# Attention 2: one slot for the keys and values of both token tiles, the key turn one slot sooner, weight transfers behind three swaps

## The reference

```python
x = x + _layernorm(_L0_attn_ref(_layernorm(x, axis=-1), ...), axis=-1)
x = x + _layernorm(_L0_ffn_ref(_layernorm(x, axis=-1), ...), axis=-1)

# in _L0_ffn_ref, for hidden states of 4 batches x 256 tokens x 256:
q = (h @ Wq).reshape(B, S, NH, HD)       # NH = 32 query heads of HD = 128
k = (h @ Wk).reshape(B, S, KVH, HD)      # KVH = 4 key heads
v = (h @ Wv).reshape(B, S, KVH, HD)
q = _rope(q, pos)                        # x1*cos - x2*sin, x1*sin + x2*cos on the two halves
k = _rope(k, pos)
scores = jnp.einsum('bqhd,bkhd->bhqk', q, k) / jnp.sqrt(jnp.float32(HD))   # k, v repeated for 8 query heads each
attn = jax.nn.softmax(where(causal, scores, -1e9), axis=-1)
o = jnp.einsum('bhqk,bkhd->bqhd', attn, v).reshape(B, S, NH * HD) @ Wo
# then: router, top 8 of 32 experts, gated experts and a shared expert
```

## Time and profile before

| | |
|---|---|
| time, median of 3 runs | 948.99 us (947.24 to 949.40) |
| profiled execution, its own time | 950.87 us |
| span of the profiled execution | 948.8 us |
| busy share of the span: PE, PEld, DVE, ACT, POOL | 91%, 85%, 65%, 60%, 48% |
| attention 2: start of its program, first scores, scores of slot 60 | 184.2, 200.45, 598.55 us |
| mean granted TensorE clock | 0.97 |

### The profile page before, as it was taken

The page is one execution under the profiler, slowest core; times in us unless marked ns, Lnnn a source line. Parts: engine busy times, 40 slices in busy tenths (PEclk is TensorE's granted clock), DMA queues, the critical chain, the costliest instruction groups (busy, mean ns, idle before and its releaser), DMA issues. The chain is left out here.

```text
span 948.8 us, 18792 instructions
## 1 busy us (share of the span) xinstructions
PE 867.5 (91%) x6108; PEld 802.1 (85%) x6108; DVE 616.5 (65%) x1620; ACT 570.5 (60%) x1570; POOL 455.9 (48%) x486
## 2 busy tenths in 40 slices
PE   5799998767999999999999999978999999999994
PEld 4699897657999998999899999867888888888884
DVE  5456667647787787778777777755444544544546
ACT  6788888656766766667666667654333333433333
POOL 3743334357867766777776777720222222221221
PEclk9799999978999999999999999997999999999998
DMA  7001000131114111421111111200433333333321
GB/s 234 1 1 46 22 23 1 59 93 39 35 46 142 38 45 35 114 66 46 34 46 35 46 45 36 51 1 18 144 116 116 114 98 115 101 114 116 112 82 45
DMA packets 50246, 63.34 MB, mean 67 GB/s; under 512 B 5728, under 2 KB 36064, under 8 KB 50176
## 3 DMA queue, kind: packets, MB, share of 16 engines
q1 hardware_dynamic: 49088, 61.41, 22.2%
q10 hardware_dynamic: 1088, 1.05, 0.3%
HBM read 41.86 MB, written 1.18 MB: 45 GB/s over the span
## 5 line engine op out<-in xcount | busy, mean ns | idle before, releaser
L639 POOL TENSOR_TENSOR b_prob<-b_prob,b_rsum 128x256 f32<-128x256 f32 (+1 forms) x128 | 104.7, 839 | 108.3 <-DVE b_rsum L621 108.3
L73 PE MATMUL banks<-act_t,b_w 128*128 128x256 f32 (+1 forms) x392 | 129.3, 330 | 3.9 <-DVE b_work L1194 2.8
L74 PE MATMUL banks<-act_t,b_w 128*128 128x256 f32 (+1 forms) x392 | 127.2, 324 | 0.0
L75 PE MATMUL banks<-act_t,b_w 128*128 128x256 f32 (+1 forms) x392 | 127.0, 324 | 0.0
L1955 ACT ACTIVATE moe_hid<-banks 128x512 fp32r<-128x512 f32 x66 | 39.5, 598 | 124.1 <-DVE banks L2046 124.1
L1355 ACT ACTIVATE b_prob<-banks,b_negmax 128x128 f32<-128x128 f32 (+1 forms) x256 | 103.6, 416 | 13.3 <-DVE b_negmax L1342 12.9
L2039 DVE TENSOR_TENSOR moe_gated<-banks,moe_share 128x512 f32<-128x512 f32 x66 | 45.6, 691 | 85.0 <-PE banks L75 80.9
L1211 ACT ACTIVATE b_qt<-b_work 128x512 fp32r<-128x512 f32 x64 | 40.5, 632 | 97.5 <-POOL b_work L1206 97.5
L639 POOL TENSOR_TENSOR a_prob<-a_prob,a_rsum 128x256 f32<-128x256 f32 x64 | 52.0, 834 | 82.2 <-DVE a_rsum L621 82.2
L1206 POOL TENSOR_TENSOR b_work<-b_work 128x512 f32<-128x512 f32 x64 | 86.7, 1355 | 9.2
L1202 POOL TENSOR_TENSOR b_work<-b_work,rope_t 128x512 f32<-128x512 f32 x64 | 84.2, 1315 | 8.2 <-DMA b_work<-b_work 8.2
(11 more groups left out here) (237 smaller groups left out, 3026.0 us busy)
## 6 DMA issues: line engine op xcount, KB each, us to landing
b_work<-b_work SPq DMA_DIRECT2D x128, 128.0 KB, 2.3
moe_share<-gates SPq DMA_DIRECT2D x32, 512.0 KB, 3.6
b_w_raw<-in_b_wq SPq DMA_DIRECT2D x4, 1024.0 KB, 5.5
b_w_raw<-in_b_wo SPq DMA_DIRECT2D x4, 1024.0 KB, 9.6
...
```

Of the source, the lines that this page charges most:

```text
L73: nc.tensor.matmul(out, w_lo, m_hi, start=start, stop=False, skip_group_check=skip)
L74: nc.tensor.matmul(out, w_hi, m_lo, start=False, stop=False, skip_group_check=skip)
L75: return nc.tensor.matmul(out, w_hi, m_hi, start=False, stop=stop, skip_group_check=skip)
L639: last = self.m.nc.gpsimd.tensor_tensor(rows, rows, rsum[:, :, t:t + 1].to_broadcast([PART, 2, width]), ALU.mult)
```

## The change

Keys and values of both token tiles are projected together in slot 0, into the two halves of one bank. They are copied out by two ACT instructions over both tiles instead of four, and multiplied by the cosines by one DVE instruction instead of two. POOL does its part in slot 1, ahead of the rotation of the queries and no longer behind it, with two `b_k_sin` instructions and one `b_k_row` over both tiles. PE turns the keys in slot 2 instead of slot 3, and their split moves along. The weights of a group are split from slots 4, 6, 8 and 10 instead of 1, 4, 7 and 10. The transfer of the weights for group 1 is issued by SP behind the first three swaps. In the diff the removed bodies of the old functions, which stand above, are shortened.

```diff
-    KV0, KV1, KT = range(3)
-    KV_AT = {0: KV0, 1: KV1}
-    KT_AT = 3
-    ROPE_AT = {1: KV0, 2: KV1}
+    KV, KT = range(2)
+    KV_AT, ROPE_AT, KT_AT = 0, 1, 2
     SWAPPED = 32
-    SPLIT_AT = {1: 0, 4: 1, 7: 2, 10: 3}
+    SPLIT_AT = {4: 0, 6: 1, 8: 2, 10: 3}
...
+    def pe_kv(self, pe, it):
+        nc, bank = self.m.nc, self.m.qt_ps
         wait(pe, self.w_ready, 4 * (it // NB) + 3)
+        wait(pe, self.kt_ready, it)
         if it < NB:
             wait(pe, self.join.turn.lo_done, it + 1)
-        if u == self.KV0:
-            wait(pe, self.kt_ready, it)
-        elif it:
-            wait(pe, self.k_raw_ready, NTT * it + 1)
-        for c in range(NC):
-            at = c * B_QKV + HPI * DH
-            last = three(nc, bank[:, 0:2 * DH], self.src(it, 0, c, t * PART, PART),
-                         self.src(it, 1, c, t * PART, PART), self.w_at(it, 0, at, 2 * DH),
-                         self.w_at(it, 1, at, 2 * DH), c == 0, c == NC - 1)
+        for t in range(NTT):
+            for c in range(NC):
+                at = c * B_QKV + HPI * DH
+                last = three(nc, bank[:, t * 2 * DH:(t + 1) * 2 * DH], self.src(it, 0, c, t * PART, PART),
+                             self.src(it, 1, c, t * PART, PART), self.w_at(it, 0, at, 2 * DH),
+                             self.w_at(it, 1, at, 2 * DH), c == 0, c == NC - 1)
         last.then_inc(self.kv_full, 1)
...
+    def kv_rows(self, i):
+        return self.m.qt_ps[:].rearrange("p (t i n) -> p t i n", t=NTT, i=2)[:, :, i, :]
...
+        wait(act, self.kv_full, 2 * it + 1)
+        wait(act, self.rotated, it)
+        nc.scalar.activation(self.k_raw[:], self.kv_rows(0), ACT.Copy).then_inc(self.k_raw_ready, 1)
...
+        nc.scalar.activation(self.values(it, 0, NTT).rearrange("p (t n) -> p t n", t=NTT), self.kv_rows(1),
+                             ACT.Copy).then_inc(self.v_raw, 1)
...
+    def dve_kv(self, dve, it):
+        wait(dve, self.k_raw_ready, it + 1)
+        wait(dve, self.rotated, it)
+        self.m.nc.vector.tensor_tensor(self.k_cos[:], self.k_raw[:], self.m.rope[:, 2, :, :],
+                                       ALU.mult).then_inc(self.k_cos_ready, 1)
+
+    def pool_kv(self, pool, it):
...
+        halves = lambda x: x.rearrange("p t (a d) -> p t a d", a=2)
+        wait(pool, self.k_raw_ready, it + 1)
+        for t in range(NTT):
+            last = nc.gpsimd.tensor_tensor(halves(self.k_sin[:])[:, t], halves(self.k_raw[:])[:, t, ::-1, :],
+                                           halves(self.m.rope[:, 3, :, :])[:, t], ALU.mult)
+        last.then_inc(self.k_sin_ready, 1)
+        wait(pool, self.k_cos_ready, it + 1)
+        wait(pool, self.k_sin_ready, it + 1)
+        wait(pool, self.kv_full, 2 * it)
+        nc.gpsimd.tensor_tensor(self.k_row[:], self.k_cos[:], self.k_sin[:], ALU.add).then_inc(self.rotated, 1)
+
+    def pe_kt(self, pe, it):
+        nc, bank = self.m.nc, self.m.qt_ps
+        wait(pe, self.rotated, it + 1)
+        wait(pe, self.k_raw_ready, it + 1)
+        wait(pe, self.v_raw, it + 1)
+        for t in range(NTT):
+            last = nc.tensor.transpose(bank[:, t * PART:(t + 1) * PART], self.k_row[:, t, :], self.m.ident[:])
+        last.then_inc(self.kv_full, 1)
+
+    def act_kt(self, act, it):
+        wait(act, self.kv_full, 2 * it + 2)
+        wait(act, self.s_full, 2 * PAIRS * (it - 1))
+        self.m.nc.scalar.activation(self.keys(it, 0, SEQ), self.m.qt_ps[:, 0:SEQ], ACT.Copy).then_inc(self.kt_hi, 1)
+
+    def dve_kt(self, dve, it):
+        wait(dve, self.kt_hi, it + 1)
+        self.m.nc.vector.tensor_tensor(self.keys(it, 1, SEQ), self.m.qt_ps[:, 0:SEQ],
+                                       self.keys(it, 0, SEQ).bitcast(F32), ALU.subtract).then_inc(self.kt_ready, 1)
...
-        if it + 1 < self.ITS and p in self.KV_AT:
-            self.pe_kv(pe, it + 1, self.KV_AT[p])
+        if it + 1 < self.ITS and p == self.KV_AT:
+            self.pe_kv(pe, it + 1)
         if self.runs(P - 5):
             self.pe_project(pe, *self.at(P - 5))
         if self.runs(P - 4):
             self.pe_values(pe, *self.at(P - 4))
         if it + 1 < self.ITS and p == self.KT_AT:
-            self.pe_kv(pe, it + 1, self.KT)
+            self.pe_kt(pe, it + 1)
...
+        if it + 1 < self.ITS and p == self.ROPE_AT:
+            self.pool_kv(pool, it + 1)
         if self.runs(P + 2):
             self.pool_rotate(pool, P + 2)
-        if it + 1 < self.ITS and p in self.ROPE_AT:
-            self.pool_kv(pool, it + 1, self.ROPE_AT[p])
...
-            load_weights(1)
             for P in range(self.STAGES):
                 slot = P - 3
+                if slot == 0:
+                    load_weights(1)
                 if slot > 0 and slot % (PAIRS * NB) == 13 and slot // (PAIRS * NB) < KV - 2:
                     load_weights(slot // (PAIRS * NB) + 2)
                 self.sp_swap(sp, P)
...
-            self.pe_kv(pe, 0, self.KV0)
-            self.pe_kv(pe, 0, self.KV1)
+            self.pe_kv(pe, 0)
             self.pe_queries(pe, 0)
             self.pe_queries(pe, 1)
-            self.pe_kv(pe, 0, self.KT)
+            self.pe_kt(pe, 0)
             self.pe_queries(pe, 2)
...
-                pe.wait_ge(*((self.raw_ready, 2) if b == 2 else (self.k_raw_ready, NTT)))
+                pe.wait_ge(self.raw_ready, 2)
```

More of the change, by code:

```diff
@@ L1218, in dve_queries @@
                                        ALU.subtract).then_inc(self.qt_ready, 1)
-    def kv_bank(self, it, u):
-        m = self.m
-        return m.y_ps if it == 0 and u == self.KV1 else m.qt_ps
-    def pe_kv(self, pe, it, u):
-        nc = self.m.nc
-        bank = self.kv_bank(it, u)
-        if u == self.KT:
-            wait(pe, self.rotated, NTT * it + NTT)
-            wait(pe, self.k_raw_ready, NTT * it + NTT)
-            for t in range(NTT):
-                last = nc.tensor.transpose(bank[:, t * PART:(t + 1) * PART], self.k_row[:, t, :], self.m.ident[:])
-            last.then_inc(self.kv_full, 1)
-            return
-        t = u
+    def pe_kv(self, pe, it):
+        nc, bank = self.m.nc, self.m.qt_ps
@@ L1249, in pe_kv, with act_kv @@
         last.then_inc(self.kv_full, 1)
-    def act_kv(self, act, it, u):
+    def kv_rows(self, i):
+        return self.m.qt_ps[:].rearrange("p (t i n) -> p t i n", t=NTT, i=2)[:, :, i, :]
+    def act_kv(self, act, it):
         nc = self.m.nc
-        bank = self.kv_bank(it, u)
-        wait(act, self.kv_full, 3 * it + u + 1)
-        if u == self.KT:
-            wait(act, self.s_full, 2 * PAIRS * (it - 1))
-            nc.scalar.activation(self.keys(it, 0, SEQ), bank[:, 0:SEQ], ACT.Copy).then_inc(self.kt_hi, 1)
-            return
-        wait(act, self.v_ready, it - 1)
-        nc.scalar.activation(self.values(it, u, 1), bank[:, DH:2 * DH], ACT.Copy).then_inc(self.v_raw, 1)
-        wait(act, self.rotated, NTT * it + u - 1)
-        nc.scalar.activation(self.k_raw[:, u, :], bank[:, 0:DH], ACT.Copy).then_inc(self.k_raw_ready, 1)
@@ L1264, in dve_kv @@
-    def dve_kv(self, dve, it, u):
-        nc = self.m.nc
-        if u == self.KT:
-            wait(dve, self.kt_hi, it + 1)
-            nc.vector.tensor_tensor(self.keys(it, 1, SEQ), self.kv_bank(it, u)[:, 0:SEQ],
-                                    self.keys(it, 0, SEQ).bitcast(F32),
-                                    ALU.subtract).then_inc(self.kt_ready, 1)
-            return
-        wait(dve, self.k_raw_ready, NTT * it + u + 1)
-        wait(dve, self.rotated, NTT * it + u - 1)
-        nc.vector.tensor_tensor(self.k_cos[:, u, :], self.k_raw[:, u, :], self.m.rope[:, 2, u, :],
-                                ALU.mult).then_inc(self.k_cos_ready, 1)
@@ L1298, in act_values @@
     def act_values(self, act, it):
-        wait(act, self.v_raw, NTT * (it + 1))
+        wait(act, self.v_raw, it + 1)
         wait(act, self.pv_done, PAIRS * it)
@@ L1481, in slot_act @@
             self.act_exp(act, p, P)
-        if it + 1 < self.ITS and p in self.KV_AT:
-            self.act_kv(act, it + 1, self.KV_AT[p])
+        if it + 1 < self.ITS and p == self.KV_AT:
+            self.act_kv(act, it + 1)
         if self.runs(P - 4):
@@ L1486, in slot_act @@
         if it + 1 < self.ITS and p == self.KT_AT:
-            self.act_kv(act, it + 1, self.KT)
+            self.act_kt(act, it + 1)
         if self.runs(P + 3):
@@ L1504, in slot_dve @@
             self.dve_normalise(dve, (P - 1) % PAIRS, P - 1)
-        if it + 1 < self.ITS and p in self.KV_AT:
-            self.dve_kv(dve, it + 1, self.KV_AT[p])
+        if it + 1 < self.ITS and p == self.KV_AT:
+            self.dve_kv(dve, it + 1)
         if self.runs(P - 4):
@@ L1614, in _ @@
             join.act_input(act, 2)
-            self.act_kv(act, 0, self.KT)
+            self.act_kt(act, 0)
             join.norm_f.roots(act, 3)
@@ L1658, in _ @@
             self.dve_cos(dve, 1)
-            self.dve_kv(dve, 0, self.KT)
+            self.dve_kt(dve, 0)
             join.norm_f.factors(dve, 3)
```

23 lines of the change are left out of this document (4 added, 19 removed).

## The result

| | before | changed |
|---|---|---|
| time, median of 5 runs each | 948.33 us (947.24 to 949.40) | 953.98 us (949.18 to 955.48) |
| ratio | | 1.0058, interval 1.0041 to 1.0075 |
| profiled execution, its own time | 950.87 us | 949.18 us |

The change makes the kernel 0.6% slower. The forecast was 952.3 and slower.

The account below looks back on a forecast made before the run. PE was taken to set plain iterations (25.53 us), POOL's closed ring the groups with weights (105.3). Start -6.3 plus iterations' loss +9.9 gave +3.6, rounded to +3.3 on 948.99: 952.3 us, range 944.5 to 957.

Parts of the forecast that it names:

- The ring gets the keys: Forecast case in attention 2: POOL's keys work lengthens slot 1's turn to 7.6 us; total 952.3, chance 0.50.
- the ring: Attention 2's closed cycle: POOL normalises and rotates queries, ACT and DVE split them, DVE's reciprocal frees POOL; 6.08 us a turn.
- Iteration and groups: Attention 2: 25.95 us without weights (25.53 before), 109.7 per four-iteration group (107.6), 83.75 for iterations 1 to 3 (79.23).
- The steady loss: Iterations of attention 2 after its start: 9.9 us lost together, between 3 and 12.
- Quarters: Weight quarters split by DVE in slots 1 and 3: add 1.0 us in slot 1, 2.45 in slot 3.
- The start: Start of attention 2, first swap ahead of the weights: first scores 4.9 us sooner, total gain 6.3 (5 to 8.5).
- Cosines on DVE: DVE's double-width cosine product of the keys lengthens slot 0's turn by 0.75 us above 5.9 (bounds 0.1 and 1.1).
- PE's waits: Sign: PE's idle time would stand ahead of the first scores of slots 3 and 0, waiting for DVE's `b_qt`.
- Both waits of the earlier trace go.: PE's idle times ahead of the keys' turn (0.68 us) and the next iteration's first scores (0.33) disappear.
- Rival 4: PE waiting at the keys was independent of the ring; removal gives 13.6 us, the start 6; about 930, chance 0.07.
- no DMA wait of more than 3 us: Sign at the start of attention 2: first scores near 195.5, no such wait ahead of POOL's first rotation.
- The scores of slot 4: Refutation sign in attention 2: the prediction is wrong if these scores are not at least 5 us sooner.

Follow-up runs that it names:

- e3: Changed kernel with POOL's sine products behind slot 1's rotation, addition behind slot 2's rotation, turn of the keys in slot 3; 944.98 us, ratio 0.996.
- e9: Changed kernel with POOL's work on the keys behind the rotation of slot 1 instead of ahead, turn still in slot 2; 956.63 us, ratio 1.008.
- e4: Changed kernel once more, unchanged, for a second profile; 954.49 us, ratio 1.0052.
- e7: Changed kernel with the weight quarters on DVE in slots 5, 6, 9 and 10 instead of 5, 7, 9 and 11; 949.66 us, ratio 1.0019.
- e11: Changed kernel with DVE's cosine product of the keys cut to 2 columns per token tile in all iterations but the first; 950.56 us, ratio 1.0029.
- e5: Changed kernel with the keys' cosine product at the end of DVE's slot 0 program, ahead of the addition to `acc`; 962.68 us, ratio 1.0147.
- e6: Changed kernel with only the turn of the keys back in slot 3; 968.51 us, ratio 1.0209.
- e12: Changed kernel with POOL's keys work behind slot 0's rotation, turn in slot 2, quarters in slots 5, 6, 9 and 10; 934.60 us, ratio 0.9856.

## Why the prediction was right, and where its sizes were off

- *The ring gets the keys.* Right in place and size: 7.6 for slot 1's turn and 7.55 measured, 5.9 for a plain one and 5.85 to 6.01. e3 and e9 take the keys off the ring and its turn falls to 5.86 and 6.24.
- *Iteration and groups.* 25.95 forecast, 25.94 measured; 109.7 and 109.7; 83.75 for the three iterations and 83.5 between normalisations. The steady loss was put at 9.9; in the traces it is 10.0 (first profile) and 10.4 (e4).
- *Quarters.* 1.0 forecast for slot 1, 1.1 measured; 2.44 for slot 3, 2.36 measured. The give-back of 0.5 behind a late quarter is in e7's turns.
- *The start.* This is the term that was mis-sized. 6.3 was taken. The first profile has just that (slot 4's normalisation 41.16 us after the start of attention 2 for 47.47), but in other parts than forecast, which is luck: 3.4 us up to the first scores for the 4.9, then 1.8 up to the first normalisation, where none was forecast and where the profile before had its granted clock of 0.50 (193.0 to 206.7) and this one 1.00, then 1.1 up to slot 4 for 1.9. There POOL's turn of slot 1 is 8.39 and not 7.6, and 0.62 us of it is a wait for the fourth swap, for which the forecast had 1 us at most. The second profile has 5.3 in all, with a low clock at the start that the forecast had priced at "a half to a whole us". The load's share by the times is 3.9. The second profile's start and steady loss explain 1.5 us of the difference between +3.3 and the +5.7 measured. The rest lies outside the stretches of attention 2 read here and wasn't settled.
- *Cosines on DVE.* The size was right (6.54 for the 6.65 forecast) but its cause only partly. The step "outputs, cosine product, addition and maxima stand behind it in DVE's queue" is true, but making the product 0.26 us shorter makes the turn only 0.1 shorter (e11). In the rows of slot 0 ACT's `b_ot`, behind its two copies of the keys, is ready at 527.99, only 0.22 before DVE gets to it: without the product, ACT's queue would give nearly the same slot. In iteration 11 of e11, where the product takes 0.16, DVE does wait 0.60 us for it. That ACT's copies are this second limit was read from the rows; no run moved them.
- *PE's waits.* The forecast had them ahead of the scores of slots 3 and 0. In slot 3 they are there, but only in iterations with a late ring (1.1 us idle in iterations 6 and 10, none in 12), and ahead of slot 0's there are none. The one ahead of slot 1's projection, for the addition to `acc`, was missed. Its end shows it: PE starts 0.1 us after that addition in the changed kernel, in e5 and in e11, and moving the product in front of it made it longer (e5).
- *"Both waits of the earlier trace rows go."* True (no idle time at the turn of the keys from iteration 2 on), but treated as worth nothing. e6 shows that the earlier turn is worth 14.5 us, given the keys on the ring. The change had put the keys on the ring and at the same time moved the turn out of its reach; the forecast sum, made from the turns of the ring alone, was right because the second had been done.
- *Rival 4, "the keys were the cause, about 930".* False for this change, since it moved the keys onto the ring. But e12 reaches 934.6 with the keys off the ring, ready early, the same load and quarters in slots 1 and 2: most of the gain that the rival named was there to be had, by another placement. The places of the quarters alone gave 4.3 of it (e7).
- *The bounds.* The upper end of the range, 957, is 1 us above its own sum (948.99 - 5 + 12 = 956.0); nothing hangs on it. Of the signs, "no DMA wait of more than 3 us" ahead of POOL's first rotation did not come: it is 3.58, since POOL gets there before the swap is issued. The scores of slot 4 come 8.0 us sooner after the start of attention 2 (7.1 in e4), where the prediction would have been wrong under 5.
